# A graph layer with a long sort: edge chain four turns earlier, receiver rows spread, table split moved off GpSimd

## What is computed

```python
dst, src = edge_index
edge_feat = concatenate([h[dst], h[src], rel_pos, distance], axis=-1)
x = silu(edge_feat @ W1 + b1)
x = silu(x @ W2 + b2)
scores = (x @ W3 + b3)[:, 0]
mx = segment_max(scores, dst, num_segments=num_nodes)
exp_scores = exp(scores - mx[dst])
den = segment_sum(exp_scores, dst, num_segments=num_nodes)
alpha = exp_scores / (den[dst] + EPS)
msg = h[src] @ Wv * (alpha * node_weight[src])[:, None]
out = x_in + h + segment_sum(msg, dst, num_segments=num_nodes)   # x_in is h
return layernorm(out, axis=-1)
```

## Time and profile before

| | |
|---|---|
| median of 3 runs | 926.76 us (926.49 to 930.16) |
| the profiled execution | 929.5 us, span 927.7 us |
| PE, DVE, ACT, GpSimd (POOL) busy | 707.7, 640.9, 548.5, 597.2 us |
| DMA traffic | 188.46 MB, mean 203 GB/s |
| longest idle time of GpSimd | 84.1 us, for `kg_t` (the sort) |
| granted TensorE clock, mean | 0.924 of full speed |

### The profile page before, as it was taken

The page is one execution under the profiler, slowest core; times in us unless marked ns, Lnnn a source line. Parts: engine busy times, 40 slices in busy tenths (PEclk is TensorE's granted clock), DMA queues, the critical chain, the costliest instruction groups (busy, mean ns, idle before and its releaser), DMA issues.

```text
span 927.7 us, 13366 instructions
## 1 busy us (share of the span) xinstructions
PE 707.7 (76%) x3718; PEld 485.4 (52%) x3718; DVE 640.9 (69%) x2264; ACT 548.5 (59%) x1280; POOL 597.2 (64%) x624
## 2 busy tenths in 40 slices
PE   0001388879998898999898988788999999999610
PEld 0000254546555565666566756566676677666510
DVE  8997788868677676788778978864544454455824
ACT  0000056777667688677677967886665665676440
POOL 3000577777777777777777543467777777775677
PEclk9999998979999999999899988889999999999765
DMA  6000348999999899999999999975443333322131
GB/s 234 0 0 0 67 100 298 316 336 348 325 343 317 295 329 346 327 338 306 289 322 312 321 261 261 293 220 159 111 119 104 95 96 106 106 75 60 65 82 46
DMA packets 120370, 188.46 MB, mean 203 GB/s; under 512 B 21147, under 2 KB 80182, under 8 KB 120296
## 3 DMA queue, kind: packets, MB, share of 16 engines
q1 hardware_dynamic: 86536, 97.47, 35.0%
q0 software_dynamic: 19648, 38.74, 14.8%
q10 hardware_dynamic: 14112, 51.39, 14.5%
HBM read 109.89 MB, written 77.76 MB: 202 GB/s over the span
## 4 chain that ended last, share of the span: by engine, by line
PE 42%; DVE 23%; POOL 11%; DMA 9%; issue 8%; ACT 5%; SPq 1%; ACTq 0%; DVEq 0%; POOLq 0%
PE bank L723 13%; POOL out_rows L446 11%; DMA xin<-in_x 6%; DVE dst L979 4%; PE bank L710 3%; PE bank L665 3%; PE bank L653 3%; PE bank L697 3%; PE bank L690 3%; DMA out_rows<-xin 3%; ACT xin L509 3%; DVE region L786 3%; PE bank L662 3%; PE bank L663 3%; PE bank L644 3%
## 5 line engine op out<-in xcount | busy, mean ns | idle before, releaser
L509 ACT ACTIVATE xin<-xin,drs 128x128 f32<-128x128 f32 x736 | 290.2, 480 | 198.0 <-DVE drs L961 192.0
L442 POOL DMA_INDIRECT hk<-in_x,kg_t x196 | 187.4, 956 | 143.6 <-DVE kg_t L870 84.1
L723 PE MATMUL bank<-hk 128*125 128x512 bf16 x1032 | 247.4, 400 | 7.3 <-DVE snd_i L1036 4.5
L442 POOL DMA_INDIRECT rec<-in_xw,snd_i x196 | 186.2, 950 | 101.6 <-issue 56.7
L446 POOL DMA_INDIRECT out_rows<-hk,sidx_t x196 | 191.0, 975 | 68.9 <-issue 57.3
L723 PEld LDWEIGHTS bank<-hk 128*125 128x125 bf16 x1032 | 147.3, 145 | 99.2 <-issue 21.7
L979 DVE BATCH_NORM_STATS2 dst<-xin 128x6 f32<-128x256 f32 x392 | 135.1, 410 | 7.0 <-DMA xin<-in_x 7.0
L1021 DVE TENSOR_SCALAR hk<-hk,rid 128x512 bf16<-128x512 f16 x344 | 108.9, 378 | 0.1
L558 ACT ACTIVATE hk<-hk,ers 128x128 f32<-128x128 f32 x196 | 79.7, 481 | 0.9 <-DVE ers L961 0.9
L1088 DVE TENSOR_TENSOR hk<-bank,hk 128x512 f32<-128x512 f32 x49 | 33.4, 682 | 65.0 <-PE bank L690 64.9
L710 PE MATMUL bank<-wsel,hk 125*128 125x5 f32 x344 | 46.9, 260 | 35.6 <-DVE hk L1028 35.6
(11 more groups left out here) (203 smaller groups left out, 1004.6 us busy)
## 6 DMA issues: line engine op xcount, KB each, us to landing
xin<-in_x SPq DMA_DIRECT2D x98, 512.0 KB, 7.4
out_rows<-xin ACTq DMA_DIRECT2D x98, 512.0 KB, 6.4
rec_d<-rec SPq DMA_DIRECT2D x49, 258.0 KB, 8.2
region<-rec_d SPq DMA_DIRECT2D x49, 258.0 KB, 4.8
hk<-vc_d SPq DMA_DIRECT2D x43, 256.0 KB, 5.8
krow<-seg_d SPq DMA_DIRECT2D x49, 128.0 KB, 3.9
hk<-in_x,kg_t POOLq DMA_INDIRECT x196, 5.2
rec<-in_xw,snd_i POOLq DMA_INDIRECT x196, 6.0
```

The costliest lines, as they stand in the source:

```text
L442: pool.indirect_dma_start(out=to, out_offset=None, in_=frm, in_offset=bass.IndirectOffsetOnAxis(ap=index, axis=0)).then_inc(done, 16)
L509: ins = nc.scalar.activation(xin[:, j % X_RING, n, :], xin[:, j % X_RING, n, :], ACT.Identity, bias=drs[:, j // 4 % 2, 1, c:c + 1], scale= ...
L723: ins = pe.matmul(bank[7][0:SEL, :], tab[:, k, n, 0:SEL], oh[:, k, :], start=(k == 0 and n == 0), stop=(k == CH - 1 and n == PIECES - 1))
```

## The change

- `E_FROM` 9 becomes 5: 50 parts of the edge chain lie in the looks, turn 43 has part 2 of step 16 alone, and step 17 begins in turn 44.
- `write_rec(g)` moves from turn g + 7 to turn 3 + 45g // 49 (`rec_turn`). The waits for the rows' flags and `tab_ready`, the first `load_rec` and `load_far` stand in turn E_FROM - 1 behind the dense loads, not ahead of them.
- GpSimd's order: three hk first; the other 36 of the first 39 evenly among the 49 hs; the `rt` of a taken group five groups ahead of it, each handed over by itself (`take_gathered(k, g)`, in the turn behind the look that comes before it).
- The one-hots of look 0 stand inside `sort()`, ahead of line 896; the last transpositions (`last_flip`) and the copies of their results (`last_columns`) move to turn 1. `load_places(1)` goes ahead of the rows' flags on SP. The PSUM banks of the transpositions are others.
- The table split leaves GpSimd: ACT copies a piece to bf16, PE subtracts it from the value in PSUM by a matmul with the negated identity, ACT copies the rest as the next piece.

Changed PSUM banks and moved helpers are left out below.

```diff
 HK_LOW = 39
-LEAD = 4
-REC_LAG = 7
-E_FROM = 9
+LEAD = 3
+REC_LAG = 3
+E_FROM = 5
+RT_AHEAD = 5
...
+def rec_turn(g):
+    return REC_LAG + g * (LOOKS + 2) // G
 def pool_plan():
-    order = [("hk", g) for g in range(LEAD)] + [("rt", k) for k in range(len(TAKEN))]
+    order = [("hk", g) for g in range(LEAD)]
+    done = LEAD
...
         order.append(("hs", g))
-        if g + LEAD < HK_LOW:
-            order.append(("hk", g + LEAD))
-    order += [("hk", g) for g in range(HK_LOW, G)]
+        for k, t in enumerate(TAKEN):
+            if max(0, t - RT_AHEAD) == g:
+                order.append(("rt", k))
+        while done < HK_LOW and done - LEAD < (HK_LOW - LEAD) * (g + 1) // G:
+            order.append(("hk", done))
+            done += 1
+    order += [("hk", g) for g in range(done, G)]
...
             load_places(0)
+            load_places(1)
...
             for i, now in enumerate(TURNS):
-                if i + 1 < LOOKS:
+                if 2 <= i + 1 < LOOKS:
                     load_places(i + 1)
-                if i == E_FROM - 1:
-                    sp.wait_ge(S["rows_out"], 80)
-                    sp.wait_ge(S["tab_ready"], 1)
-                    load_rec(0)
-                    for b in range(2):
-                        load_far(b)
...
                     load_block(2 * (i + 1))
-                if 0 <= i - REC_LAG < G:
-                    write_rec(i - REC_LAG)
+                for g in range(G):
+                    if rec_turn(g) == i:
+                        write_rec(g)
...
                     load_block(2 * (i + 1) + 1)
+                if i == E_FROM - 1:
+                    sp.wait_ge(S["rows_out"], 80)
+                    sp.wait_ge(S["tab_ready"], 1)
+                    load_rec(0)
+                    for b in range(2):
+                        load_far(b)
...
-            pool.wait_ge(S["pay_in"], 32)
-            cut(nc.gpsimd.tensor_copy(payf[:, :, 0, :], snd_f), 1)
-            cut(nc.gpsimd.tensor_copy(tab[:, :, 0, 0:SEL], whole), 2)
-            cut(nc.gpsimd.tensor_tensor(payr, whole, tab[:, :, 0, 0:SEL], ALU.subtract), 3)
-            cut(nc.gpsimd.tensor_copy(tab[:, :, 1, 0:SEL], payr), 4)
-            cut(nc.gpsimd.tensor_tensor(payr, payr, tab[:, :, 1, 0:SEL], ALU.subtract), 5)
-            cut(nc.gpsimd.tensor_copy(tab[:, :, 2, 0:SEL], payr), 6)
...
                 elif kind == "rt":
-                    if g == 0:
-                        pool.wait_ge(S["tab_ready"], 1)
+                    pool.wait_ge(S["tab_ready"], 1)
...
                     wait(pool, "pay_ready", looks(g))
-                    if g == TAKEN[0]:
-                        pool.wait_ge(S["rt_ready"], 1)
+                    if g in TAKEN:
+                        pool.wait_ge(S["rt_ready"], TAKEN.index(g) + 1)
...
         def _(act):
...
+            act.wait_ge(S["w_in"], 16 * 12)
+            act.wait_ge(S["pay_in"], 32)
+            nc.scalar.activation(away[:], ident[:], ACT.Copy, scale=-1.0).then_inc(S["pieces"], 1)
+            nc.scalar.activation(payf[:, :, 0, :], snd_f, ACT.Copy).then_inc(S["pieces"], 1)
+            act.wait_ge(S["pieces"], 2)
+            nc.scalar.activation(tab[:, :, 0, 0:SEL], flat, ACT.Copy).then_inc(S["pieces"], 1)
+            for n in range(1, PIECES):
+                act.wait_ge(S["left"], n)
+                for h in range(2):
+                    ins = nc.scalar.activation(tab[:, 4 * h:4 * h + 4, n, 0:SEL],
+                                               bank[h][:, 0:4 * SEL].rearrange("p (k n) -> p k n", k=4), ACT.Copy)
+                ins.then_inc(S["pieces"], 1)
...
+            for n in range(PIECES - 1):
+                pe.wait_ge(S["pieces"], n + 3)
+                for h in range(2):
+                    if n == 0:
+                        pe.matmul(bank[h][:, 0:4 * SEL], ident[:], flat[:, 4 * h:4 * h + 4, :], start=True, stop=False,
+                                  skip_group_check=True)
+                    ins = pe.matmul(bank[h][:, 0:4 * SEL], away[:], tab[:, 4 * h:4 * h + 4, n, 0:SEL], start=False, stop=True,
+                                    skip_group_check=True)
+                ins.then_inc(S["left"], 1)
...
                 ins.then_inc(S["flip_done"], 1)
-            pe.wait_ge(S["flip_ready"], 7)
-            for h in range(2):
...
-            for k, name in enumerate(("sidx", "seg")):
+            pe.wait_ge(S["pieces"], 5)
+            def last_flip():
+                pe.wait_ge(S["flip_ready"], 7)
                 for h in range(2):
-                    o = k * T + h * SROWS
...
-            ins.then_inc(S["flip_done"], 1)
-            pe.wait_ge(S["wz_in"], 16)
-            pe.wait_ge(S["consts"], 2)
-            pe.wait_ge(S["tab_split"], 1)
-            pe.wait_ge(S["tab_ready"], 1)
...
+                for k, name in enumerate(("sidx", "seg")):
+                    for h in range(2):
+                        o = k * T + h * SROWS
+                        ins = pe.transpose(bank[6][:, o:o + SROWS], row[name][0:SROWS, h * P:(h + 1) * P],
...
+                ins.then_inc(S["flip_done"], 1)
+                pe.wait_ge(S["wz_in"], 16)
+                pe.wait_ge(S["consts"], 2)
...
                     if s in TAKEN:
-                        pe.wait_ge(S["rt_ready"], 1)
+                        pe.wait_ge(S["rt_ready"], TAKEN.index(s) + 1)
...
             for i, now in enumerate(TURNS):
+                if i == 1:
+                    last_flip()
                 if i == E_FROM:
+                    pe.wait_ge(S["tab_ready"], 1)
...
+            def last_columns():
+                dve.wait_ge(S["flip_done"], 7)
+                vec.tensor_copy(by_row(idx_t[:]), halves(bank[5][:, 0:T]))
+                vec.tensor_copy(by_row(kcol[:]), halves(bank[6][:, T:2 * T]))
+                link(vec.scalar_tensor_tensor(out=by_row(sidx_t[:]), in0=by_row(idrel), scalar=float(N + 1),
+                                              in1=halves(bank[6][:, 0:T]), op0=ALU.add, op1=ALU.min))
+                dve.sem_inc(S["tab_ready"], 1)
...
                             dve.wait_ge(S["flip_done"], n + 1)
...
                 dve.wait_ge(S["flip_done"], 5)
...
                 link(vec.tensor_tensor(same, same, row["sidx"], ALU.max))
+                one_hot(0, 0, EARLY)
+                one_hot(0, EARLY, CH)
...
                 handed()
-                dve.wait_ge(S["flip_done"], 7)
-                vec.tensor_copy(by_row(idx_t[:]), halves(bank[7][:, 0:T]))
-                vec.tensor_copy(by_row(kcol[:]), halves(bank[6][:, T:2 * T]))
-                link(vec.scalar_tensor_tensor(out=by_row(sidx_t[:]), in0=by_row(idrel), scalar=float(N + 1),
-                                              in1=halves(bank[6][:, 0:T]), op0=ALU.add, op1=ALU.min))
-                dve.sem_inc(S["tab_ready"], 1)
...
-            sort()
-            dve.wait_ge(S["split"], 6)
-            dve.sem_inc(S["tab_split"], 1)
-            dve.wait_ge(S["w_in"], 16 * 12)
-            link(vec.tensor_scalar(wvh[:], wvh[:], 0.5, None, ALU.mult))
-            dve.sem_inc(S["consts"], 1)
...
+            sort()
+            link(vec.tensor_scalar(wvh[:], wvh[:], 0.5, None, ALU.mult))
+            dve.sem_inc(S["consts"], 1)
...
-            def take_gathered():
-                dve.wait_ge(S["rt_in"], 16 * TPG * len(TAKEN))
-                for k, g in enumerate(TAKEN):
-                    vec.tensor_copy(efs[:, g, :].rearrange("p (q w) -> p q w", q=TPG), rt[:, k, :, 1:WORDS])
-                    ins = vec.tensor_copy(snd_i[:, g * TPG:(g + 1) * TPG], rt[:, k, :, 0].bitcast(I32))
-                ins.then_inc(S["rt_ready"], 1)
+            def take_gathered(k, g):
+                dve.wait_ge(S["rt_in"], 16 * TPG * (k + 1))
+                vec.tensor_copy(efs[:, g, :].rearrange("p (q w) -> p q w", q=TPG), rt[:, k, :, 1:WORDS])
+                vec.tensor_copy(snd_i[:, g * TPG:(g + 1) * TPG], rt[:, k, :, 0].bitcast(I32)).then_inc(S["rt_ready"], 1)
...
                     take_places(i - 1)
-                one_hot(i, 0, EARLY)
+                if i > 0:
+                    one_hot(i, 0, EARLY)
...
                     take_words(i - 1)
-                one_hot(i, EARLY, CH)
-                if i == REC_LAG:
-                    take_gathered()
+                if i > 0:
+                    one_hot(i, EARLY, CH)
+                if i == 1:
+                    last_columns()
+                for k, g in enumerate(TAKEN):
+                    if looks(g) + 1 == i:
+                        take_gathered(k, g)
...
                     (part_one, part_two, part_three)[part](s)
```

More of the change, by code:

```diff
@@ L263, in gnn_kernel @@
         S = {n: sem(n) for n in (
-            "key_in", "t_in", "w_in", "wz_in", "pay_in", "split", "tab_split", "setup", "consts",
+            "key_in", "t_in", "w_in", "wz_in", "pay_in", "pieces", "left", "setup", "consts",
             "flip_ready", "flip_done", "kg_ready", "vc_ready", "vc_out", "tab_ready", "rows_ready", "rows_out", "fix_in",
@@ L595, in _ @@
```

(42 more changed lines are left out.)

15 lines of the change are left out of this document (6 added, 9 removed).

## The result

| | before | after |
|---|---|---|
| median (range), 20 runs each on the same chips | 927.05 us (918.33 to 936.10) | 932.49 us (926.02 to 939.49) |
| the profiled execution, its span | 929.5, 927.7 us | 931.33, 929.5 us |
| ratio after/before, 95% interval | | 1.0062 (1.0039 to 1.0084) |

The change made the kernel slower by 0.6%, 5.7 us, where 10.3 us less were forecast. So the traces tell where time went, and the ratio what it cost.

What follows compares the result with a forecast made beforehand. Bounds: DVE's sort, then PE and transfers close together in the looks, then PE, which also sets the closing GpSimd scatters. Front -10.2, looks +7.8, records +3.0, tail -10.9 sum to -10.3: 926.8 to 916.5 us, range 904 to 928.

Steps and rivals of the forecast that it cites:

- Parts 1 and 2: Ahead of the first selection: table split off GpSimd (5.6 us) and first one-hots inside the sort's decoding (4.7); 10.2 us taken.
- Rival E: Front gain fails: first one-hots wait for the broadcast, or DVE's stall had another cause; 924 us, chance 0.05.
- Part 3: Edge chain from turn 5: +7.8 us in the looks, -10.9 us in the tail.
- Part 4: Receivers spread, records at turn 3 + 45g/49: SP held at write_rec delays second dense loads; +3 us, bounds 0 and +14.
- my turn lengths: Turns of the looks: 8.61 us without edge parts, 10.15 with the first edge parts, 10.55 with fuller steps.
- Rival D: Turns 3 to 42: SP and GpSimd held by turns, losses not made up; 10.76 us per edge turn, 928 us; chance 0.12.
- Rival C: Transfers bound the looks: 2.9 MB more there costs 9 us on top of the main sum, 925.5 us; chance 0.13.

Runs made afterwards that it cites:

- e2: Kernel before with the table split on ScalarE and PE, first one-hots inside the decoding and late transpositions; records, order and edge chain as before: 918.04 us, 0.9891.
- e1: Kernel before with only the table split moved from GpSimd to ScalarE and PE: 922.4 us, 0.9924.
- e15: e9 with the records of group 1 and groups 3 on one more turn later, up to three turns behind the changed kernel's: 918.17 us, 0.9887.
- e16: e6 with records up to three turns later than in the changed kernel: 912.75 us (5 runs), 0.9848.
- e3: Changed kernel with E_FROM = 9 again, all else as changed: 935.95 us, 1.0082.
- e9: e6 with the edge chain from turn 9 (E_FROM = 9): 931.19 us, 1.0033.
- e6: e4 with the first read-back (load_rec, load_far) ahead of the dense loads of turn 4: 917.55 us, 0.9893.
- e11: Changed kernel with only the first read-back moved ahead of the dense loads of turn 4: 926.78 us, 0.9989.
- e4: Changed kernel with the records of groups 2 to 48 written two turns later: 925.03 us, 0.9954.
- e7: Changed kernel with every record written one turn earlier: 952.17 us, 1.0268.
- e5: e4 with the edge chain from turn 9 (E_FROM = 9): 938.0 us, 1.0107.
- e13: e2 with the receiver rows spread evenly among the sender rows on GpSimd: 919.33 us, 0.9864.

## Why the prediction failed, step by step

**Parts 1 and 2 were right.** Forecast -10.2, measured -10.1 (e2); first selection forecast at 107.0, seen at 107.1. The split alone: -5.5 in e1's trace, -7.1 in its ratio (interval 4.0 to 10.1), forecast -5.6. No sort instruction shares time with GpSimd any more. Two minima of the same form, at nearly the times of those in the earlier trace rows that took 0.99 and 2.09 us, in the changed kernel's timeline:

```profile
7.34 0.27 DVE L837 TENSOR_TENSOR region<-region 128x64 f32<-128x64 f32 x1
8.47 0.22 DVE L837 TENSOR_TENSOR region<-region 128x64 f32<-128x64 f32 x1
```

The split on ScalarE and PE ended before 20 us and nobody waited for it; its cover, the sort, held. Rival E is out.

**Part 3: the sum came out where records are late enough, its two terms did not.** Forecast: 4 x 8.61 + 16 x 10.15 + 22 x 10.55 - 421.2 = +7.8 in the looks and -10.9 in the tail, -3.1 in all. E15 to e16, both with three turns' slack, give -3.6 us, but the interval is some 4 us to either side and holds zero too. In their traces the looks got 4.5 us shorter (426.8 to 422.3), not 7.8 longer, and the tail up to the rows of group 16 5.5 us shorter (110.1 to 104.6), not 10.9. The changed kernel's tail looks like a hit, 102.6 against 115.1, but e2, with the chain still from turn 9, has 110.0: 5.1 of its 12.5 us have nothing to do with E_FROM. So the agreement is luck in part. It also isn't one number: by the ratios the same step is worth 1.9 us (e3 to the change), 13 (e9 to e6) and 3.6 (e15 to e16). The rows' addition of group 16 in the timelines of e2, e15 and e16, where turn 43 begins at 531.92, 533.52 and 529.15:

```profile
641.88 0.69 DVE L1112 TENSOR_TENSOR hk<-bank,hk 128x512 f32<-128x512 f32 x1 [3.33 <-PE bank L711]
```

```profile
643.66 0.69 DVE L1115 TENSOR_TENSOR hk<-bank,hk 128x512 f32<-128x512 f32 x1 [3.37 <-PE bank L716]
```

```profile
633.75 0.69 DVE L1115 TENSOR_TENSOR hk<-bank,hk 128x512 f32<-128x512 f32 x1 [3.40 <-PE bank L716]
```

**Part 4 is the step that failed**, +3 with bounds 0 and +14. By the ratios, one edit at a time: -10.1 (front, e2), -0.4 (spread, records up to three turns later than in the change, e15), -3.6 (edge chain, e16), +4.2 (records a turn earlier, e6), +8.9 (two turns earlier still, e11), +6.8 (read-back behind the loads, the change). The sum is the measured +5.7 by construction, but for rounding, each term is good to some 4 us, and in another order of edits the shares differ: with the chain from turn 9, all of part 4 costs 17.7 us (e2 to e3). What it shows is that part 4 costs 18 to 20 us, not 3, and over its upper bound of 14. Two faults of the argument are in it:

- I counted when each group's gathers are there and when SP comes to its record, found them "level all through", and priced level at +3. With the chain from turn 5, level is not free: two more turns gain 10.0 us (the change to e4) and 8.9 (e11 to e6), both clear of their intervals, one turn less costs 19 (e7), and e4, e6 and e16 have no wait for gathers at all. The way by which it costs is argued: a hold delays the second dense load of its turn, as in the chain of waits above. E3 and e5 speak against that as the only way, as there 62.1 us of holds went and no time with them.
- I noted that `load_rec(0)` "now stands behind two loads" and gave it no price. It had one: 8.9 us to land, from an issue at the very end of turn 4, for PE instructions at the head of turn 5 that stand ahead of the look's words. In the looks of the changed kernel turn 5 alone is 9.4 us over its 10.15. Turns 6 to 8 gave 5.4 us of that back (187.1 - 162.0 = 25.1 for three turns against 30.5), and the turns that follow are 6.6 us too long up to turn 25 and 5.0 up to turn 43, against my turn lengths.

**Rival D was the right one.** With its 10.76 us a turn the looks come to 421.2 + 7.8 + 14.4 = 443.4 us; they took 445.6, 10.80 a turn from 5 to 43 ((552.64 - 142.41) / 38), over the 10.7 that I had named as the sign of a wrong prediction. With my front and tail D gives 929.5 - 10.2 + 22.2 - 10.9 = 930.6 for the profiled execution, which took 931.33. What was wrong is its chance, 0.12. I held against it that GpSimd's own pace is no slower than the turns'. The count was short: `pool_plan()` has 364 gathers behind the first 12, not 360, which makes 10.2 us a turn beside turns of 10.15. And equal pace says that a delay doesn't grow; it also says that it isn't made up, as the gathers of group 20 in e11 and in the changed kernel show, 7.5 us apart. And D's place was half right: much of its loss was in one turn that I didn't name.

**Rival C is out as the cause of the loss.** E16 moves the same 188.46 MB as the change, only three records (0.8 MB) fewer of them in the looks, and from turn 9 to 25 does so at a DMA share of 1.00 and 332 GB/s, above the 0.96 and 314 of the change. At that share the transfers may well be what bounds e16 there. Why the share of the change is lower is not settled by held loads: e5, without any, has 0.95 and 310. The Trainium skill's figure for such transfers (SBUF — State Buffer, Summary: rules for kernel authors), about 358 GB/s, was still not reached over a stage; 334, in e13, is the most seen here in turns 9 to 25.

**Smaller signs.** `kg_t` was there for GpSimd's first gather at 92.58 (forecast 93.4). Turn 9 came at 187.1 (180 to 186), turn 43 at 552.6 (536 to 541), the first scatter at 651 (625 to 635): each late by what turn 5 and the holds took. Ten groups of scatters at the end: as forecast.

**What stays open.** Why the holds cost with the chain from turn 5 and not with it from 9 (e3, e5) is open. Between records two and three turns later SP waits for gathers in neither, yet e6 to e16 is 4.2 us (intervals overlap a little) and e9 to e15 13.5 us, well outside. In the traces DVE's waits for x are 13.0 us in e9 and 6.3 in e15. But these are single executions, and e9's is one of its fastest. That a record's own landing, now close to a dense load of the same turn, delays it, is a guess; no run separates it. Nor is it shown why with E_FROM = 9 the first two turns bring nothing (e3 to e5) and the third 13.5 us, while with 5 the first two bring 9 to 10 and the third some 4.

## What to carry to other kernels

In a queue that issues in program order, price each transfer by what stands behind it while it waits, and count the slack of every entry up to its landing: "level" with its producer can cost, and here three more turns of slack and the first read-back ahead of the loads turned a loss of 0.6% into a gain of 1.5%. The first read-back of a chain that is started earlier needs its own look: who reads it first, how many loads stand ahead of it, and which other work stands behind the reader on its engine. When two engines run at the same pace without slack, a single stall on one can be passed on and not recovered, as GpSimd's in turn 5. A term whose number comes out should be looked up in the trace too: part 3's did, with both of its halves off.

## What the chip showed beside that

The granted TensorE clock while the sort runs. The window from 20 to 90 us, in the kernel before, the changed kernel and e6 (columns as in the earlier trace rows; the clock is the third number from the end):

```profile
20.00:90.00 70.00, 2.73 (x8) 1.16 (x8) 62.37 (x265) 0.00 (x0) 0.00 (x0) 1.00 0.03 11
```

```profile
20.00:90.00 70.00, 2.76 (x8) 1.16 (x8) 62.28 (x251) 0.00 (x0) 0.00 (x0) 0.50 0.03 12
```

```profile
20.00:90.00 70.00, 2.75 (x8) 1.15 (x8) 62.29 (x251) 0.58 (x2) 0.00 (x0) 1.00 0.03 12
```

PE does the same eight transpositions in all three. Before, it had done nothing ahead of them, and the clock shown is 1.00, the level of 2.4 GHz. In the other two it had split the table between 12 and 20 us, with the same instructions; the changed kernel then shows 0.50, the level of 1.2 GHz, for the whole stretch, and e6 shows 1.00. So the same work goes with either level, and no run here says what decides. The mean clock of an execution tells them apart: of the changed kernel's 20 runs, 16 have 0.86 to 0.87 and 4 have 0.91 to 0.92. It cost nothing that can be told: those 4 took 930.3 to 935.7 us, within the 926.0 to 939.5 of the others, and the first look's 24 matmuls were busy 6.96 us in the changed kernel, 8.11 in e6 and 7.35 before.

A kernel on one core can also spread more than three runs show: the first three of the kernel before agreed within 0.4%, its 20 runs lie between 918 and 936 us.
